# Float32 partial shifts of a grouped convolution on TensorE: four turns of eight tiles of 64 columns in place of three turns of sixteen tiles of 32

## What is computed

```python
    def _L0_cond_ref(x, c, weight, c_weight, bias):
        N, C_IN, L = (32, 128, 2048)
        C_OUT, K, GROUPS = (128, 9, 4)
        C_DIM, PAD, STRIDE = (128, 4, 1)
        out = lax.conv_general_dilated(x, weight, window_strides=(STRIDE,), padding=[(PAD, PAD)],
                  dimension_numbers=('NCH', 'OIH', 'NCH'), feature_group_count=GROUPS)
        ctx = jnp.einsum('nd,od->no', c, c_weight)
        return out + ctx[:, :, None] + bias[None, :, None]
...
    x = x + _L0_cond_ref(x, cond_128, L0_cond_weight, L0_cond_c_weight, fside_S_0)
    x = x + _L1_cond_ref(...)
    x = x + _L2_cond_ref(...)
    x = x + _L3_cond_ref(...)
```

## Time and profile before

| | |
|---|---|
| Median of 3 runs | 632.58 us (632.04 to 632.8) |
| Profiled execution: its time | 635.33 us |
| Profiled execution: its span, first to last instruction | 633.5 us |
| TensorE busy | 622.8 us, 98% of the span |
| VectorE, ScalarE, GpSimd busy | 79%, 53%, 43% |
| Mean granted TensorE clock | 0.991 of full speed |

### The profile page before, as it was taken

One profiled execution on the slowest core, in us unless ns is written; L12 is line 12 of the kernel. 1 busy time (PEld: TensorE's weight loads), 2 busy tenths in 40 slices (PEclk: granted clock), 3 DMA queues, 4 the chain that ended last, 5 costly groups with the idle time before them and its releaser, 6 DMA issues.

```text
span 633.5 us, 26750 instructions
## 1 busy us (share of the span) xinstructions
PE 622.8 (98%) x11938; PEld 506.3 (80%) x11938; DVE 500.9 (79%) x1002; ACT 338.2 (53%) x626; POOL 272.3 (43%) x163
## 2 busy tenths in 40 slices
PE   8999999999999999999999999999999999999995
PEld 6888897777788777889877778777878877788874
DVE  6899777978777887887887887797877788788735
ACT  4665455555455456455456446555545545645534
POOL 4133454354355345355435345435435534534220
PEclk8999999999999999999999999999999999999998
DMA  8066665557765556775555776555776555655515
GB/s 244 24 188 215 203 211 177 204 163 225 232 207 156 190 176 199 232 232 158 173 191 175 232 232 182 158 202 162 223 232 208 155 190 176 201 169 168 161 76 201
DMA packets 50572, 118.84 MB, mean 188 GB/s; under 512 B 5621, under 2 KB 26282, under 8 KB 42714
## 3 DMA queue, kind: packets, MB, share of 16 engines
q1 hardware_dynamic: 49170, 116.04, 58.1%
q0 software_dynamic: 576, 1.26, 0.5%
q10 hardware_dynamic: 776, 0.89, 0.4%
HBM read 35.33 MB, written 33.55 MB: 109 GB/s over the span
## 4 chain that ended last, share of the span: by engine, by line
PE 96%; DMA 2%; DVE 1%; ACT 1%; issue 0%; ACTq 0%; DVEq 0%
PE ps L1068 45%; PE ps L1079 19%; PE ps L1090 16%; PE ps L1214 14%; PE ps L1192 1%; DMA out_sb<-in_L_cond_weight 1%; DMA out_planes<-out_taps 1%; ACT out_sb L740 1%; PE ps L1262 0%; PE ps L1185 0%; DVE out_taps L856 0%; DVE x_in L950 0%; DVE x_hi L993 0%; PE ps L1250 0%; PE ps L1302 0%
## 5 line engine op out<-in xcount | busy, mean ns | idle before, releaser
L513 POOL COPY out_sb<-out_planes 128x2048 f32<-128x2048 f32 x30 | 123.0, 4099 | 187.8 <-issue 162.0
L496 POOL COPY x_full<-x_in 128x2048 f32<-128x2048 f32 x29 | 117.1, 4038 | 113.9 <-DVE x_lo L822 110.1
L846 DVE SCALAR_TENSOR_TENSOR z_lo<-ps,bias_tab,z_hi 128x1024 fp32r<-128x1024 f32 x62 | 76.7, 1279 | 60.7 <-ACT z_hi L649 60.7
L1090 PE MATMUL ps<-x_full,taps_raw 32*32 32x512 f32 x2880 | 102.2, 598 | 0.0
L1068 PEld LDWEIGHTS ps<-z_hi,taps_hi 32*128 32x128 f32 x1488 | 71.0, 183 | 35.4 <-issue 25.1
L1068 PE MATMUL ps<-z_hi,taps_lo 32*128 32x512 f32 x1488 | 96.5, 387 | 0.0
L836 DVE SCALAR_TENSOR_TENSOR y_lo<-ps,bias_tab,y_hi 128x512 fp32r<-128x512 f32 x128 | 87.2, 744 | 10.2 <-ACT y_hi L639 10.2
L1068 PE MATMUL ps<-z_hi,taps_hi 32*128 32x512 f32 x1488 | 94.2, 396 | 0.0
L657 ACT ACTIVATE out_taps<-ps,bias_tab 128x512 f32<-128x512 f32 x62 | 39.3, 685 | 102.2 <-PE ps L1068 102.2
L1068 PE MATMUL ps<-z_lo,taps_hi 32*128 32x512 f32 x1488 | 90.3, 385 | 0.0
L1214 PE MATMUL ps<-y_hi,mix_w 32*128 32x512 f32 x1024 | 88.0, 385 | 0.0
(11 more groups left out here) (158 smaller groups left out, 831.0 us busy)
## 6 DMA issues: line engine op xcount, KB each, us to landing
x_in<-in_x SPq DMA_DIRECT2D x31, 1024.0 KB, 5.3
out_planes<-out_taps SPq DMA_DIRECT2D x122, 256.0 KB, 3.6
out<-out_sb SPq DMA_DIRECT2D x30, 1024.0 KB, 4.6
mix_w<-prod SPq DMA_DIRECT2D x124, 128.0 KB, 4.0
x_in<-in_x SPq DMA_DIRECT2D x2, 512.0 KB, 5.9
out<-out_sb POOLq DMA_DIRECT2D x2, 512.0 KB, 3.5
out<-x_full SPq DMA_DIRECT2D x7, 128.0 KB, 2.9
out_taps<-in_L_cond_weight SPq DMA_DIRECT2D x1, 512.0 KB, 5.8
```

What stands on the lines that cost most here:

```text
L496: pool.tensor_copy(row_order(t, d, x[:, :, home(t, d)]), x_order(t, d, x_in[t.par(d)][:, :])).then_inc(x_planed, 1)
L513: pool.tensor_copy(x_order(t, d, out_sb[t.par(d)][:, :]), row_order(t, d, out_planes[:, :, :]))\
L846: dve.scalar_tensor_tensor(out=z_home(t, 0)[1][:, 2 * h:2 * h + 2, home(t, 0)], in0=ps[:, k:k + 2, :], scalar=bias_tab[:, b, 2 * G:BIAS], ...
L1090: tile = pe.matmul(ps[rows(p), first_bank + g, :], taps_raw[l][rows(g), d - p, :], full[rows(g), d % PH, c:c + S], start=False, stop=(n == ...
```

## The change

The six partial shifts are laid on tiles of 32 rows by 64 columns. A tile holds two neighbouring phases; where a shift touches only one of them, the weights of the other are zeros. The eight pairs of shift and phase pair that are needed make four turns with eight tiles each (two tiles for each of the four groups). So a sample has 32 float32 multiplies in place of 48, and four turns in place of three. The weights stand in a new buffer, `taps_full`, which GpSimd clears and fills with six small copies of `taps_raw` near the start; TensorE waits for it once, before the first convolution of sample 2.

```diff
+TILES = (((0, 0, 2), (2, 2, 4)), ((1, 0, 2), (9, 2, 4)), ((2, 0, 2), (10, 2, 4)), ((9, 0, 2), (11, 2, 4)))
...
+        taps_full = sb("taps_full", [C, 2 * PARTIAL, C])
...
+            pool.memset(taps_full[:, :, :], 0.0).then_inc(taps_full_zeroed, 1)
+            pool.wait_ge(taps_full_zeroed, 1)
+            pool.wait_ge(taps_raw_step[0], 2)
+            for p in range(PH):
+                if p < PARTIAL:
+                    last = pool.tensor_copy(taps_full[:, p:PARTIAL, rows(p)], taps_raw[0][:, 0:PARTIAL - p, :])
+                if p > 0:
+                    last = pool.tensor_copy(taps_full[:, PARTIAL:PARTIAL + p, rows(p)], taps_raw[0][:, TAPS - p:TAPS, :])
+            last.then_inc(taps_full_done, 1)
             spread_first()
...
-            def partial_turns(first_bank, l, full, done, step):
-                for n in range(PARTIAL):
+            def partial_turns(first_bank, full, done, step):
+                for n, tiles in enumerate(TILES):
                     for g in range(G):
-                        for p in range(PH):
-                            d = n if p <= n else n + TAPS
-                            c = step * (d // PH)
-                            tile = pe.matmul(ps[rows(p), first_bank + g, :], taps_raw[l][rows(g), d - p, :],
-                                             full[rows(g), d % PH, c:c + S], start=False, stop=(n == PARTIAL - 1))
-                        if n == PARTIAL - 1:
+                        for d, p, q in tiles:
+                            c, o = step * (d // PH), slice(GC * p, GC * q)
+                            tile = pe.matmul(ps[o, first_bank + g, :], taps_full[rows(g), d if d < PARTIAL else d - TAPS + PARTIAL, o],
+                                             full[rows(g), d % PH, c:c + S], start=False, stop=(n == len(TILES) - 1))
+                        if n == len(TILES) - 1:
                             tile.then_inc(done, 1)
...
+                if t.at(FIRST_MIXED):
+                    pe.wait_ge(taps_full_done, 1)
```

More of the change, by code:

```diff
@@ L169, in conditioned_residual_kernel @@
         taps_raw_step = [sem(f"taps_raw_step{l}") for l in range(2)]
+        taps_full_done = sem("taps_full_done")
+        taps_full_zeroed = sem("taps_full_zeroed")
         taps_hi_done = [sem(f"taps_hi_done{l}") for l in range(2)]
@@ L1117, in conv0_mixed @@
                     middle()
-                partial_turns(bank(t, 0), 0, full, conv0_done, step)
+                partial_turns(bank(t, 0), full, conv0_done, step)
             def conv0(t, turns=range(TURNS)):
```

## The result

The changed kernel takes 640.95 us (median of 3 runs, 640.84 to 642.44) against 632.58: a ratio of 1.0141, 95% interval 1.0116 to 1.0166 (the ratio is worked out from all the runs; the two medians alone give 1.0132). The forecast was 641.3.

What follows compares the result with a forecast made beforehand. TensorE was taken to bound the kernel, 18.82 us a sample. The partial turns would take 0.48 + 2.58 + 0.05 + 0.52 = 3.63 us against 3.34, +8.7 us in 30 samples: 632.6 + 8.7 = 641.3 us, range 638.5 to 654.

Steps and rivals of the forecast that it cites:

- What bounds: Whole kernel: TensorE sets the pace, 18.82 us a sample; no other engine does until more than 3 us are gone.
- The reach: Partial turns: a load beyond 64 instructions waits for the oldest unfinished one to end; eight-tile turns escape this; 64%, 641.3 us.
- first rival: Partial turns: loads keep program order when a tile's buffer is full; +0.56 us a sample, 649.5 us; chance 14%.
- second rival: Partial turns: the 0.19 us stall is a price of column tiles, whatever their count; +1.0 us a sample, 663 us; 13%.
- The terms: One sample's partial turns: 0.48 + 2.58 + 0.05 + 0.52 = 3.63 us against 3.34, +0.29 us a sample.
- First pass: First turn of the partial turns, weights not yet there: 0.454 + 0.027 = 0.481 us with 64-column tiles.
- upper bound of 0.440: Longest expected float32 pass on 64-column tiles, in us; six passes 2.64, giving +0.35 us a sample (+10.5 us).
- next kind: From the partial turns' last start to the first multiply of what follows: drain and switch, 0.52 us, as before.
- Faster: Partial turns: a shorter pass on 64-column tiles; streaming as float32r would give -1.2 us a sample, 597 us; chance 4%.
- cheaper switch: Around the partial turns: drain and switch shrink with half as many column tiles; +0.10 us a sample, 635.6 us; 5%.
- Edits at nothing: Near the start: GpSimd's clearing and copies, under 3.2 us, are hidden; TensorE's new wait finds its semaphore set.

Runs made afterwards that it cites:

- e5: Changed kernel with partial turns as two turns of eight 64-column tiles, then one of sixteen 32-column tiles (32 multiplies): 626.74 us, ratio 0.9929 to the kernel before.
- e3: Changed kernel with the 48 multiplies of before on 32-column tiles, as four turns of twelve tiles: 651.66 us.
- e8: Changed kernel with the 48 multiplies on 32-column tiles, three turns of eight on one half of the phases, then three on the other: 673.68 us.
- e1: Changed kernel with the three turns of sixteen 32-column tiles of before, weights from taps_full (the preparation alone): 632.74 us, ratio 1.0006 to the kernel before.
- e12: e5 with the product in the last convolution one whole turn later (21 turns ahead of it, not 20): 623.82 us, ratio 0.9868 to the kernel before.
- e11: e5 with the product in the last convolution four whole turns later (24 turns ahead of it, not 20): 635.04 us, ratio 1.0042 to the kernel before.
- e7: e5 with the turn of sixteen 32-column tiles in the middle, between the two 64-column turns: 629.28 us.

## Why the prediction was right

**What bounds.** Right for this change: the period grew by what the block grew, 0.28 us, but for 0.02, and TensorE met no new wait for another engine. Wrong in the other direction: the prediction said that nobody else sets the pace until more than 3 us of TensorE's work were gone, because VectorE is busy 15.16 us of 18.82. In e5 TensorE's work became 0.31 us shorter, and a wait for VectorE's `y_lo` took 0.1 us of it a sample. A busy share does not show such a wait; the distance between one engine's end and the next one's start, here 0.15 us, does.

**The reach.** Right, and now shown rather than read: with durations and distances of starts from the kernel before alone, the rule gave 3.11 for the changed kernel, 3.48 for e3 and 4.20 for e8, and each came within 0.01 us. A reach of 48 or 96 would be out by 0.33 us or more in e3 and e8, and the first burst of e3, the lone load of before and the first multiply of the idle half in e8 leave 64 alone. The step of the prediction that held least proof, that loads within the reach need not keep program order, is shown by the changed kernel's own loads: all eight tiles reload in one burst, where loads in order would have fallen 0.05 us apart each turn. This ends the first rival. The second rival, a stall of 0.19 us for column tiles, is refuted by the same burst at 64 columns and by e8 at 32. (The 32 loads of turn 1, which the prediction counts as four to each row group, are eight to each, two for each tile; what it draws from them holds.)

**The terms.** First pass 0.480 (forecast 0.481), each further one 0.429 (0.43; the upper bound of 0.440, taken from 128-column tiles, did not come), last tile 0.047 after the first (0.05), from the last start to the next kind 0.517 (0.52), in all 3.62 (3.63). The load of 64 columns lasts 132 ns (130), the multiply that waits for it up to 640 (640). The forecast of the profiled execution, 644.0, was 1.6 us too high: the 2.75 us by which the profiled execution of before stands over its median came from a late start (56.2 us to the first partial turns, where e1 takes 52.8) and did not come again in that size. The median's forecast does not depend on it.

**Faster, or a cheaper switch.** Neither came. A float32 pass takes as long at 64 columns as at 32, and the switch is 0.09 us with 64-column tiles too (e5).

**Edits at nothing.** The preparation was under-sized (4.4 us for 3.2) and hidden all the same (e1).

**By page.** The queue depth of 64 that the Trainium skill states ("TensorE: Matmul & The Clock Gate", architectural detail on the 16 sub-arrays) is what e3 and e8 measured. The statement of the Trainium skill on the same page (the part on packing small matmuls) that multiplies start in program order is not what the traces show: in the changed kernel the first passes of tiles 1 to 7 start at 0.007 to 0.047 us, ahead of tile 0's second pass at 0.480, which stands before all of them in the program.

## What to carry to other kernels

When small tiles are packed into TensorE's array, count not only columns and turns but instructions until a tile comes back: two passes of float32 on sixteen tiles are 64 instructions, and then every turn waits for the oldest unfinished multiply to end, 0.2 us in 1.07. Wider tiles that carry useful columns (not zeros) halve that count at no loss: the best kernel here has the three turns of before and the 32 multiplies of the change. When such a stretch becomes shorter, look at the next wait: a third of the 8.4 us was lost to a product that stood one turn too early for VectorE (e5 against e12), and with the product three turns further still the kernel is slower than before (e11).

## What the runs showed that was not expected

- A weight load can overtake program-earlier multiplies and loads of other tiles, in the same row group or not, within a reach of 64 instructions, but no further until the oldest has ended by the trace (0.587 us after its start, plus 0.03), although its tile can start the next multiply after 0.43.
- A change of tile width inside the partial turns costs the same 0.09 us as one between column tiles and full width, and it also ends all overlap between turns: 0.19 us more for a second change (e7 against e5).
- The place of a 0.23 us product in TensorE's order was worth 3 us when it stood one turn too early and 11 us when it stood three turns too late (e5 and e11 against e12), while TensorE's busy share was 98% in all three.
